# Grouped-query self attention: values as matmul weights, scores ahead of transposes, maxima as an exponential's bias, GpSimd normalises

## The reference

```python
q = (h @ wq).reshape(B, S, NHEADS, HEAD_DIM)      # 32 heads of 64
k = (h @ wk).reshape(B, S, KVHEADS, HEAD_DIM)     # 8 heads of 64
...
g = NHEADS // KVHEADS
k = jnp.repeat(k, g, axis=2)
v = jnp.repeat(v, g, axis=2)
scores = jnp.einsum('bqhd,bkhd->bhqk', q, k) / np.float32(np.sqrt(HEAD_DIM))
causal = jnp.tril(jnp.ones((S, S), bool))
scores = jnp.where(causal[None, None], scores, jnp.float32(-1e+30))
attn = jax.nn.softmax(scores, -1)
o = jnp.einsum('bhqk,bkhd->bqhd', attn, v).reshape(B, S, NHEADS * HEAD_DIM)
x = x + o @ wo
h = _rms(x, ff_ln_w)
```

## Time and profile before

| what | value |
|---|---|
| median of 3 runs | 2782.24 us (2780.65 to 2783.71) |
| the profiled execution | 2780.92 us |
| its span, first to last instruction | 2779.2 us |
| PE busy | 2516.6 us (91%) |
| DVE, ACT, POOL busy | 1668.5, 1132.1, 932.6 us |
| mean granted TensorE clock | 0.946 |

### The profile page before, as it was taken

One profiled execution on the slowest core, in us unless ns is written; L12 is line 12 of the kernel. 1 busy time (PEld: TensorE's weight loads), 2 busy tenths in 40 slices (PEclk: granted clock), 3 DMA queues, 4 the chain that ended last, 5 costly groups with the idle time before them and its releaser, 6 DMA issues. The chain is left out here.

```text
span 2779.2 us, 48345 instructions
## 1 busy us (share of the span) xinstructions
PE 2516.6 (91%) x14891; PEld 2020.3 (73%) x14892; DVE 1668.5 (60%) x3141; ACT 1132.1 (41%) x2442; POOL 932.6 (34%) x942
## 2 busy tenths in 40 slices
PE   7999778769899989799997998998999999899998
PEld 7888655558688877578875777774665678788887
DVE  4537746669776656667675566864434325666564
ACT  2113256623343324455453133755555521444443
POOL 4213101124332235422333111753333322355555
PEclk9999889889899979899998898999999989999999
DMA  5444132125522045477774432344222031566664
GB/s 190 154 143 101 27 101 67 45 83 163 175 75 64 14 144 186 131 220 228 198 219 108 112 78 77 115 134 145 74 63 76 20 130 55 153 163 163 162 152 83
DMA packets 289277, 332.88 MB, mean 120 GB/s; under 512 B 147445, under 2 KB 202693, under 8 KB 287312
## 3 DMA queue, kind: packets, MB, share of 16 engines
q1 hardware_dynamic: 217904, 252.57, 28.9%
q0 software_dynamic: 20640, 51.74, 9.3%
q10 hardware_dynamic: 50560, 26.34, 3.3%
HBM read 233.86 MB, written 96.72 MB: 119 GB/s over the span
## 5 line engine op out<-in xcount | busy, mean ns | idle before, releaser
L898 PE MATMUL e_psum<-e_up_hi,hT_hi 128*128 x672 | 245.5, 365 | 21.3 <-DVE hT_lo L867 16.3
L900 PE MATMUL e_psum<-e_up_hi,hT_lo 128*128 x672 | 237.1, 353 | 0.0
L899 PE MATMUL e_psum<-e_up_lo,hT_hi 128*128 x672 | 236.5, 352 | 0.0
L1905 POOL TENSOR_TENSOR joint_a_p<-joint_a_p,joint_a_rinv 112x487 f32<-112x487 f32 x128 | 125.2, 999 | 196.1 <-DVE joint_a_rinv L1951 195.7
L1565 POOL TENSOR_TENSOR self_a_p<-self_a_p,self_a_mx 112x448 f32<-112x448 f32 x96 | 96.0, 1000 | 207.7 <-DVE self_a_mx L1622 207.7
L898 PEld LDWEIGHTS e_psum<-e_up_hi,hT_hi 128*128 128x128 f32 x672 | 127.7, 190 | 44.0 <-issue 32.6
L1956 DVE TENSOR_REDUCE joint_a_mx<-joint_psum 112x1 f32<-112x487 f32 x128 | 85.0, 664 | 122.1 <-PE joint_psum L1926 122.0
L794 ACT ACTIVATE e_gate<-e_psum 128x352 f32<-128x352 f32 (+1 forms) x86 | 44.4, 516 | 256.5 <-PE e_psum L900 256.0
L873 DVE TENSOR_TENSOR hT_lo<-e_psum,hT_hi 128x256 fp32r<-128x256 f32 (+2 forms) x138 | 55.6, 434 | 142.1 <-ACT hT_hi L812 142.1
L1656 ACT ACTIVATE self_a_p<-self_a_p 112x448 f32<-112x448 f32 x128 | 71.6, 575 | 165.7 <-POOL self_a_p L1565 115.4
L900 PEld LDWEIGHTS e_psum<-e_up_hi,hT_lo 128*128 128x128 f32 x672 | 127.6, 190 | 11.5
(11 more groups left out here) (565 smaller groups left out, 7419.9 us busy)
## 6 DMA issues: line engine op xcount, KB each, us to landing
e_up_raw<-in_L_ffn_w SPq DMA_DIRECT2D x64, 512.0 KB, 5.0
e_up_raw<-in_L_ffn_w SPq DMA_DIRECT2D x64, 352.0 KB, 3.7
e_dn_raw<-in_L_ffn_w SPq DMA_DIRECT2D x16, 1024.0 KB, 5.5
q_all<-p_p_t_stage ACTq DMA_DIRECT2D x56, 256.0 KB, 2.3
e_dn_raw<-in_L_ffn_w SPq DMA_DIRECT2D x16, 512.0 KB, 4.0
x_q<-q_all SPq DMA_DIRECT2D x8, 896.0 KB, 5.1
v_ctx<-front_c_v_stage SPq DMA_DIRECT2D x24, 250.0 KB
x_others<-k_ctx SPq DMA_DIRECT2D x8, 750.0 KB, 4.9
```

What stands on the lines that cost most here:

```text
L898: pe.matmul(out, lhs[0], rhs[0], start=k == 0, stop=False)
L899: pe.matmul(out, lhs[0], rhs[1], start=False, stop=False)
L900: return pe.matmul(out, lhs[1], rhs[0], start=False, stop=k == n_k - 1)
L1905: pool.tensor_tensor(p[:, r, :], p[:, r, :], rinv[:, r:r + 1].to_broadcast([T, S]), ALU.mult).then_inc(p_ready, 1)
```

## The change

A new class `GroupedSelfAttentionPart` takes the place of `SelfAttentionPart` in `self2`. The values become the weights of the last matmul (64 columns), and the transposed probabilities of an item's 4 heads become the moving side (448 columns). The two items of a step write partitions 0 to 63 and 64 to 127 of one bank. The result comes out transposed, so the transposes of `o` and the tile itself go, and `wo`'s rows are reordered on the host. The maximum is turned into `neg` on DVE and given to the exponential as its bias. There is one exponential per head, which also gives the row sum. DVE takes one reciprocal for the step's 8 heads one step later, and POOL multiplies `p` by it before the transposes. On PE a step's scores are issued ahead of the transposes of two steps before. The first batch's values are loaded without the column of ones, in whole rows.

```diff
+        def gpsimd(pool):
...
+                for i in pair(step, 1):
+                    pool.wait_ge(rinv_ready, i // W + 1)
+                    pool.tensor_tensor(p[:, i % RING, :, :], p[:, i % RING, :, :], rinv[:, i % RING, :].unsqueeze(2).to_broadcast([T, group, T]),
+                                       ALU.mult).then_inc(p_ready, 1)
...
+        def tensor(pe):
...
+                    reuse(pe, mask_done, both[-1] - N_S + 1)
+                    for j in range(group):
+                        for i in both:
+                            rows, c_k = rows_of(i), step % n_steps
+                            last = pe.matmul(ps[0:T, s_banks[i % N_S], j * T:(j + 1) * T], q[b % 2][rows, c_k * group + j, :],
+                                             k[rows, b % 2, c_k, :], start=True, stop=True)
...
+                for i in pair(step, LT):
+                    pe.wait_ge(p_ready, i + 1)
+                    reuse(pe, pt_ready, i - N_T + 1)
+                    for j in range(group):
+                        last = pe.transpose(ps[0:T, t_banks[i % N_T], j * T:(j + 1) * T], p[:, i % RING, j, :], core.ident[0:T, 0:T])
...
+                    pe.wait_ge(pt_ready, both[-1] + 1)
+                    reuse(pe, self.o_used, at - N_O + 1)
+                    for i in both:
+                        n = i % n_items
+                        last = pe.matmul(ps[rows_of(i), o_banks[at % N_O], 0:group * T], v[:, b % 2, n * dh:(n + 1) * dh],
+                                         pt[:, i % PT, :, :].rearrange("p h t -> p (h t)"), start=True, stop=True)
...
+        def vector(dve):
...
+                    dve.tensor_reduce(mx[:, i % RING, :], p[:, i % RING, :, :], AX.X, ALU.max).then_inc(mx_ready, 1)
+                    dve.wait_ge(mx_ready, i + 1)
+                    dve.tensor_scalar(neg[:, i % RING, :], mx[:, i % RING, :], -scale, None, ALU.mult).then_inc(neg_ready, 1)
+                yield
+                before = pair(step, 1)
+                if before:
+                    at = before[0] % RING
+                    dve.wait_ge(exp_done, before[-1] + 1)
+                    dve.reciprocal(rinv[:, at:at + W, :], rsum[:, at:at + W, :]).then_inc(rinv_ready, 1)
...
+        def scalar(act):
...
+                    for j in range(group):
+                        last = act.activation(p[:, i % RING, j, :], p[:, i % RING, j, :], ACT.Exp, bias=neg[:, i % RING, j:j + 1], scale=scale,
+                                              accum_out=rsum[:, i % RING, j:j + 1])
...
-                a = SelfAttentionPart(g, "a", *own_qkv(64, 32, 0.125, (0, 1), (2, 3), (4, 5), "causal", ALU.add), tiles=(q2, k2, v2))
+                a = GroupedSelfAttentionPart(g, "a", lambda b: q_all[:, tokens_of(b)], lambda b: k_all[:, tokens_of(b)], lambda b: v_all[tokens_of(b), :],
+                                             0.125, "causal", (0, 1), (2, 3), (4, 5), (q2, k2, v2))
```

More of the change, by code:

```diff
@@ L2861, with __init__ @@
 class FirstBatchPart:
-    def __init__(self, g, name, p, loads, ones=None):
-        landed, ones_set = g.sem(f"{name}_landed"), g.sem(f"{name}_ones_set")
+    def __init__(self, g, name, p, loads):
+        landed = g.sem(f"{name}_landed")
         def sync(sp):
@@ L2876, in sync @@
                         sp.wait_ge(p.v_stored[0], 16)
-                        if ones is not None:
-                            sp.wait_ge(ones_set, 1)
                 for to, src in pairs:
@@ L2883, in sync @@
             sp.wait_ge(landed, n)
[L2885 to L2892, removed]
+        g.part(name, sync=sync)
     def placed(self, order):
@@ L3348, in tokens_of @@
             return slice(b * T, (b + 1) * T)
-        def own_qkv(dh, heads, scale, *banks_and_mask):
-            return (dh, None, lambda b: q_all[:, tokens_of(b)], lambda b: k_all[:, tokens_of(b)], lambda b: v_all[tokens_of(b), :],
-                    heads, scale, *banks_and_mask)
         def head_qkv(p):
@@ L3429, in decoder @@
                     k2 = first_hi[:, :, :].bitcast(F32).rearrange("p k d -> p (k d)")[:, 0:8 * T].rearrange("p (u c t) -> p u c t", u=2, c=4)
-                    v2 = first_lo[0:T, :, :].bitcast(F32).rearrange("p k d -> p (k d)")[:, 0:2 * (8 * 65 + 128)].rearrange("p (u e) -> p u e", u=2)
+                    v2 = first_lo[0:T, :, :].bitcast(F32).rearrange("p k d -> p (k d)")[:, 0:2 * D].rearrange("p (u e) -> p u e", u=2)
                     f = FirstBatchPart(g, "f", p, [
@@ L3433, in decoder @@
                         [(k2[:, 0, :, :], k_all[:, tokens_of(0)].rearrange("(c p) t -> p c t", p=128))],
-                        [(v2[:, 0, 0:8 * 65].rearrange("p (h e) -> p h e", e=65)[:, :, 0:64], v_all[tokens_of(0), :].rearrange("t (h d) -> t h d", d=64))]],
-                        ones=v2)
+                        [(v2[:, 0, :], v_all[tokens_of(0), :])]])
                     order = ["p"] * 4 + ["p", "t", "t"] * (t.steps // 2)
@@ L3577, in laid_out @@
     ins["L0_ffn_wk"], ins["L0_ffn_wv"] = rows_first(a["L0_ffn_wk"]), rows_first(a["L0_ffn_wv"])
-    ins["L0_ffn_wo"] = pieces(a["L0_ffn_wo"])
+    ins["L0_ffn_wo"] = pieces(a["L0_ffn_wo"].reshape(4, 2, 4, 64, D).transpose(0, 2, 1, 3, 4).reshape(4 * D, D))
     ins["L0_ffn_wg"] = rows_first(a["L0_ffn_wg"])
```

101 lines of the change are left out of this document (added).

## The result

| | time, us | ratio to before, 95% interval |
|---|---|---|
| before, 3 runs | 2782.24 (2780.65 to 2783.71) | |
| changed, 3 runs | 2801.00 (2800.03 to 2801.86) | 1.0072 (1.0053 to 1.0092) |
| forecast | 2792 (2769 to 2806) | |

What follows compares the result with a forecast made beforehand. PE's list alone was taken to set the pace in `self2`. Profiled 2780.9 us, +12 for six slower sequences and -2 at the start, gave 2790.9; that execution lies 1.3 below the median, so 2792, range 2769 to 2806.

Steps and rivals of the forecast that it cites:

- The middle: Sequences 0 to 5, where ADD meets running scores: each 2.0 us slower, 29.7 us a sequence, +12 us in all.
- the forecast's own case: Whole kernel: PE stalls in the step of ADD and the clock falls behind it, 2786 to 2800, chance 0.50.
- slow exponentials: Rival: ACT's eight exponentials cost full durations and hold up copies at `wo`'s split and in light steps, +6, 2798, chance 0.12.
- unpaired halves: Rival: values matmuls on the two column halves don't run together, 1.6 us a step instead of 0.8, 2808, chance 0.08.
- PE's work that goes: PE, one sequence: transposes of `o` go and values matmuls shrink to 0.8 us a step, 22.4 us against 27.7.
- The stall: PE, step of ADD: transposes wait for DVE's late reciprocal and POOL's normalising, 3.4 to 7.2 us after scores, 3.8 us idle.
- The clock: Behind each stall PE's clock is at half for about 5.1 us, losing 2.1 us a sequence.
- The start: First scores to step 8: less PE work against slower first transposes and ACT, -2 us, between -8 and +4.
- a sign that would make things worse: In the profile after: POOL slowing beside DVE; it would prove the prediction wrong, with no size given.
- The end: After the last scores: output matmuls of the same length, 0 us, with +-1.5 for the clock.
- The clock does not hold behind the stalls: Denies the rival that the clock holds through the stalls: 2780, between 2773 and 2784, chance 0.15.
- PE stays the bound: Rival: the reciprocal's chain in the step of ADD is short enough not to stop PE, 2746 to 2772, chance 0.15.

Runs made afterwards that it cites:

- e3: Changed kernel with POOL's multiplications left out, so rows are not normalised and the transposes wait for the exponentials alone: 2758.6 us, ratio 0.9909.
- e2: Changed kernel with DVE's reciprocal ahead of a step's masks and POOL's normalising ahead of the pow of the rows' norm: 2764.7 us, ratio 0.9933.
- e11: Changed kernel with transposes and values issued three steps behind the scores instead of two, ring of eight items instead of six: 2762.0 us, ratio 0.9927.
- e1: Changed kernel with DVE's reciprocal moved ahead of a step's masks, POOL's normalising left behind the pow of the rows' norm: 2802.1 us, ratio 1.0065.
- e5: Changed kernel with 16 matmuls that nothing reads on PE ahead of the waiting transposes in the step of ADD: 2790.0 us, ratio 1.0029.
- e6: Changed kernel with one exponential an item instead of four, without bias and row sums, the reciprocal reading the maxima: 2815.8 us, ratio 1.0123.
- e8: As e2, but the reciprocal stands between the masks of a step's first and second item: 2757.8 us, ratio 0.9917.
- e12: e8 with the edit of e11 added, transposes and values one step later: 2767.1 us, ratio 0.9941.
- e9: e8 with a step's transposes put ahead of its scores on PE again: 2781.2 us, ratio 0.9994.

## Why the prediction was right, point by point

- **The number.** The middle was right, 12 us forecast for six sequences and 12.2 measured. But 2801 lies just above the 2786 to 2800 that the forecast's own case was given; it is inside the range only because that was stretched for slow exponentials and unpaired halves, and neither happened. What filled the gap is start and end, below. That part of the hit is luck.
- **PE's work that goes.** Priced at 22.4 us a sequence, measured at 23.6 (e3). The step's pieces sum as forecast outside the step of ADD: transposes 0.75, scores 0.97 and values 0.90, 2.62 in place of 0.86 + 0.97 + 0.8. The 0.90 (890.61 to 891.51) shows that the two halves of the columns do run together, since each alone is two passes of 0.40; what changing between whole and half columns costs is then within the 0.1 us above 0.8. Most of the rest is output matmuls of 2.93 for 2.87 and, in the step of ADD, 0.67 for ACT's copies, which I had put into the 3.4 us ahead of the stall but not into this sum.
- **The stall.** Each link came within 0.1 us: ADD at 2.88 (2.8 forecast) behind the end of the scores, reciprocal at 6.0 (6.0), POOL at 6.27 (6.24), transposes at 7.26 (7.2), idle 3.67 (3.8). e2, e3 and e11 each remove it in another way and each gains 36 us or more. What the prediction missed is the second lock: it had the reciprocal alone behind ADD, and e1 shows that POOL's pow would have held the normalising at the same place.
- **The clock.** Forecast: some 5.1 us at half and a loss of 2.1 a sequence. The clock falls at all six stalls, in five of them before the stall is over, and is at half for 3.1 to 6.1 us behind their ends; e5 puts the loss at 1.8. The 5.1 us from one place in `cross1` met the middle of a scatter that the prediction did not know of. The two errors of the middle, 27.8 for 27.6 and 1.8 for 2.1, nearly cancel: 29.64 against 29.7.
- **ACT.** Eight exponentials take 3.0 us a step (879.18 to 882.16), 3.2 forecast, and e6 shows that they set nothing in the middle and 0.4 us in the start.
- **The start is the term of the sum that was mis-sized**, -2 forecast and +3.5 measured. I had put PE's saving against slower transposes and ACT. e3 shows that without the normalising the start would be 48.5, close to what I forecast (49.8 - 2), and that the missing cost, 4.8 us, is the reciprocal's chain there too. PE and POOL in the start:

```profile
753.42 1.04 PE L1749 MATMUL self_psum<-x_first_hi,x_wp_lo 64*112 64x112 f32 x16 [1.12 <-DVE self_a_p L1783]
756.97 0.99 PE L1757 MATMUL self_psum<-ident,self_a_p 112*112 112x112 f32 x4 [2.51 <-POOL self_a_p L1732]
758.90 0.99 PE L1757 MATMUL self_psum<-ident,self_a_p 112*112 112x112 f32 x4 [0.94 <-POOL self_a_p L1732]
760.52 1.76 PE L1769 MATMUL self_psum<-self_a_pt,x_first_lo 112*64 112x448 f32 x4 [0.62 <-ACT self_a_pt L1805]
762.21 1.84 PE L1749 MATMUL self_psum<-x_first_hi,x_wp_lo 64*112 64x112 f32 x16
```
```profile
755.98 2.87 POOL L1732 TENSOR_TENSOR self_a_p<-self_a_p,self_a_rinv 112x448 f32<-112x448 f32 x2 [7.50 <-DVE self_a_rinv L1794]
763.40 1.82 POOL L1732 TENSOR_TENSOR self_a_p<-self_a_p,self_a_rinv 112x448 f32<-112x448 f32 x2 [4.55 <-DVE self_a_rinv L1794]
```
```profile
754.04 1.22 DVE L2172 TENSOR_TENSOR self_wo_lo<-self_w_raw,self_wo_hi 128x1024 fp32r<-128x1024 f32 x1
...
755.71 0.19 DVE L1794 RECIPROCAL self_a_rinv<-self_a_rsum 112x8 f32<-112x8 f32 x1
756.83 1.23 DVE L2172 TENSOR_TENSOR self_wo_lo<-self_w_raw,self_wo_hi 128x1024 fp32r<-128x1024 f32 x1 [0.93 <-ACT self_wo_hi L2164]
```

  The reciprocal stands behind a split of `wo` here as it stands behind ADD later. PE waits 4.6 us in three pieces, two of them for POOL, and 0.62 more for ACT's copies. From 756.4 to 770.1 the clock is at half; it had reached 1.00 at 749.6, and before the change it reached 1.00 at 751.4 and kept it. POOL's pair is also stretched beside DVE, 2.87 us for 1.82, twice in the start (at 755.98 and 772.25) and nowhere in the middle: the prediction had named this as a sign that would make things worse, and had no term for it. How the 4.8 us divide between waits, clock and this was not tried.
- **The end** was put at 0 and is +2.0. It has an ADD as well, and behind it a stall of 1.65 us and some 3 us at half clock. With the normalising early it falls to 27.5. The same step of the argument, the chain behind ADD, was counted six times where it acts seven.
- **The rivals.** The clock does not hold behind the stalls (out by the trace), the halves do run together (out by 0.90), ACT is not late (out by e6). "PE stays the bound" did not happen, but its price is right: it was to give 2746 to 2772, and the kernels that make it happen (e2, e8, e11, e12) take 2758 to 2767.

## What to carry to other kernels

Before an operation is given a new consumer, look up where its producers stand in each engine's list, all of them: here one reciprocal of 0.19 us, behind 3.1 us of other work on DVE and behind a 0.55 us operation on POOL, decided over 43 us, and moving it forward in DVE's list alone gave back nothing. Ask what work of the waiting engine lies between the start of the chain and the wait, and count that, since a step's order is worth what it covers (40 us with a late chain, 23 with an early one). And find the list's irregular step everywhere it occurs, in the first and last rounds too, not in the middle alone.

## What the runs showed of the hardware that I had not expected

- The clock can fall behind a short stall. In e9 PE was idle for 1.39 us, with 0.32 a little ahead of it, and the granted clock fell to half behind four of the six such stalls and stayed at 1.00 behind the two others. The prediction had said that from 2 us less stall on (below some 1.8) the clock would hold; here it did so twice in six. Idle of 0.67 us, once a sequence and alone in e3, left it at 1.00 from 790 to 900.
- POOL and DVE hold each other up. POOL's two multiplications take 1.82 us, and 2.87 at 755.98 of the changed kernel, where DVE's split of `wo` (1.23 us at 756.83, two operands in SBUF) falls into them. The other way round DVE's tiny operation on 4 elements takes 0.17, and 0.75 beside POOL's multiplication; DVE in e8, with POOL at work from 860.42 to 862.25:

```profile
860.07 0.17 DVE L1795 TENSOR_SCALAR self_a_neg<-self_a_mx 112x4 f32<-112x4 f32 x1
...
861.52 0.75 DVE L1795 TENSOR_SCALAR self_a_neg<-self_a_mx 112x4 f32<-112x4 f32 x1
```

  The Trainium skill, page "GPSIMD Engine Reference", section Key points, says that GpSimd shares its SBUF interfaces with VectorE and contends with instructions in a 2-port mode or with two SBUF inputs. The trace agrees: the mask, which has one of its two operands in PSUM, and the maximum, which has a single one, lost nothing beside POOL (0.57 at 860.26, 0.62 at 860.86), and the split with both operands in SBUF cost POOL 1.05 us, nearly its own length. The tiny operation has one operand in SBUF and was held up all the same, until POOL was done (861.52 + 0.75 is 862.27, POOL's end 862.24); whether it is an instruction in a 2-port mode no run here shows.
